# An attention kernel in which VectorE, not GpSimd, adds the norm's bias to the normalised rows

## What is computed

```python
def _layernorm(x, axis=-1, eps=1e-05):
    m = jnp.mean(x, axis=axis, keepdims=True)
    v = jnp.var(x, axis=axis, keepdims=True)
    return (x - m) / jnp.sqrt(v + eps)
...
    # _L0_attn_ref, on the normalised x
    tok = x.reshape(B, H * W // C, C)
...
    att = jnp.concatenate([x1, x2], axis=-1) @ proj_w + proj_b
    mu = att.mean(-1, keepdims=True)
    var = ((att - mu) ** 2).mean(-1, keepdims=True)
    normed = (att - mu) * lax.rsqrt(var + EPS) * ln_w + ln_b
    tok = tok + normed
    return jnp.transpose(tok, (0, 2, 1)).reshape(B, H, W)
...
    x = x + _layernorm(_L0_attn_ref(_layernorm(x, axis=-1), ...), axis=-1)
    x = x + _layernorm(_L0_ffn_ref(_layernorm(x, axis=-1), ...), axis=-1)
```

## Time and profile before

| | us |
|---|---|
| median of three executions | 1118.66 |
| lowest and highest | 1116.5, 1118.77 |
| the profiled execution | 1114.17 |
| its span | 1112.0 |
| TensorE (PE) busy | 932.1 |
| VectorE (DVE) busy | 890.0 |
| GpSimd (POOL) busy | 697.9 |
| ScalarE (ACT) busy | 603.9 |

### The profile page before, as it was taken

One profiled execution on the slowest core, in us unless ns is written; L12 is line 12 of the kernel. 1 busy time (PEld: TensorE's weight loads), 2 busy tenths in 40 slices (PEclk: granted clock), 3 DMA queues, 4 the chain that ended last, 5 costly groups with the idle time before them and its releaser, 6 DMA issues.

```text
span 1112.0 us, 13901 instructions
## 1 busy us (share of the span) xinstructions
PE 932.1 (84%) x4423; PEld 511.2 (46%) x4423; DVE 890.0 (80%) x1135; ACT 603.9 (54%) x907; POOL 697.9 (63%) x497
## 2 busy tenths in 40 slices
PE   5633538999889988999899988999899979889995
PEld 4432424555445544554445545454455543434442
DVE  4999997899798988899789988899889989642213
ACT  2546646655385646756475747655565635523422
POOL 2556555777479755876578756976487757632422
PEclk9856869999899999999999999999999999999997
DMA  6000310004002300023002400122002300230101
GB/s 163 22 17 3 97 37 16 16 23 115 1 1 76 95 20 0 22 73 94 0 0 75 113 0 0 48 81 59 1 1 76 77 0 1 76 76 1 38 1 38
DMA packets 78441, 45.93 MB, mean 41 GB/s; under 512 B 39616, under 2 KB 72384, under 8 KB 78400
## 3 DMA queue, kind: packets, MB, share of 16 engines
q1 hardware_dynamic: 73536, 45.10, 14.4%
q10 hardware_dynamic: 4864, 0.32, 0.3%
HBM read 28.63 MB, written 16.78 MB: 41 GB/s over the span
## 4 chain that ended last, share of the span: by engine, by line
PE 26%; DVE 26%; issue 17%; POOL 16%; ACT 13%; POOLq 0%; DVEq 0%; ACTq 0%
DVE prod L1088 10%; PE ps_gate L632 8%; PE ps_up L632 5%; PE ps_acc L656 4%; POOL sum L929 4%; PE ps_w L597 3%; POOL flo L982 3%; POOL xl L900 2%; DVE probs L1097 2%; ACT xb L736 2%; POOL o L977 2%; DVE attn L1097 2%; DVE xlo L1214 1%; POOL frs L885 1%; DVE fuse L1221 1%
## 5 line engine op out<-in xcount | busy, mean ns | idle before, releaser
L1088 DVE TENSOR_TENSOR prod<-ps_x,qkvl 128x2048 f32<-128x2048 f32 x128 | 290.5, 2282 | 8.2 <-ACT ps_x L761 7.7
L632 PE MATMUL ps_gate<-xhi,wg 128*128 128x512 f16 x512 | 198.7, 388 | 21.4 <-DVE xlo L1214 12.0
L982 POOL TENSOR_TENSOR flo<-fuse,fhi 128x512 f16<-128x512 f32 x128 | 148.9, 1166 | 92.4 <-ACT fhi L829 92.2
L632 PE MATMUL ps_up<-xhi,wu 128*128 128x512 f16 x512 | 196.3, 383 | 8.7 <-DVE fuse L1221 8.7
L632 PE MATMUL ps_gate<-xlo,wg 128*128 128x512 f16 x512 | 198.9, 388 | 0.0
L920 POOL TENSOR_TENSOR sum<-prod 128x1024 f32<-128x1024 f32 x64 | 150.7, 2361 | 75.6 <-DVE prod L1088 54.7
L632 PE MATMUL ps_up<-xlo,wu 128*128 128x512 f16 x512 | 195.7, 382 | 0.0
L929 POOL TENSOR_TENSOR sum<-prod 128x1024 f32<-128x1024 f32 x64 | 151.3, 2369 | 67.3 <-DVE prod L1088 66.2
L823 ACT ACTIVATE gact<-ps_gate,sgate 128x512 f32<-128x512 f32 x128 | 87.5, 684 | 157.3 <-PE ps_gate L632 156.9
L1221 DVE SCALAR_TENSOR_TENSOR fuse<-ps_up,sup,gact 128x512 f32<-128x512 f32 x128 | 95.4, 746 | 95.1 <-PE ps_up L632 78.8
L597 PE MATMUL ps_w<-wqkvl,xt 128*128 128x256 f32 x448 | 123.6, 401 | 24.2 <-ACT xt L743 16.5
(11 more groups left out here) (168 smaller groups left out, 1451.5 us busy)
## 6 DMA issues: line engine op xcount, KB each, us to landing
xb<-in_L_attn_x SPq DMA_DIRECT2D x64, 128.0 KB, 2.7
xr<-in_L_attn_x SPq DMA_DIRECT2D x16, 512.0 KB
attn_rows<-ratt SPq DMA_DIRECT2D x16, 512.0 KB, 3.7
o<-attn_rows SPq DMA_DIRECT2D x32, 256.0 KB, 4.2
out_x<-o SPq DMA_DIRECT2D x14, 512.0 KB
x<-in_L_ffn_w_gate SPq DMA_DIRECT2D x1, 1024.0 KB, 5.5
xr<-in_L_ffn_w_up SPq DMA_DIRECT2D x1, 1024.0 KB, 8.3
out_x<-o SPq DMA_DIRECT2D x4, 256.0 KB
```

Source lines behind the costliest of these rows:

```text
L632: mm = nc.tensor.matmul(ps[:], w[:, k, :], xs[:, k, :], start=(k == 0 and part == 0), stop=(k == KB - 1 and part == 1))
L982: nc.gpsimd.tensor_tensor(flo[:, m % SPLITS, :], fuse[:, m % 2, :], fhi[:, m % SPLITS, :], ALU.subtract).then_inc(flo_done, 1)
L1088: nc.vector.tensor_tensor(prod[:, half].rearrange("p (s j k) -> p s j k", j=WIN, k=WIN), left[:, :, None, :].broadcast_to([P, 4 * WIN, WIN ...
```

## The change

The function token_bias moves from GpSimd's block to VectorE's, with the same waits and the same semaphore at its end. Its place in the list of steps stays. VectorE comes to it where its own order has it, 16 times in all.

```diff
@@ in @block.gpsimd @@
-            def token_bias(at, bank):
-                t, g = at
-                pool.wait_ge(xn_done, WIN * t + WIN)
-                if isinstance(t, int) and at == (0, 1):
-                    pool.wait_ge(xn1_done, WIN)
-                need(pool, ratt_done, 4 * t + 2 * g - 2)
-                nc.gpsimd.tensor_tensor(xl[:, g].rearrange("p h (c t) -> p h c t", c=C),
-                                        xb[:, g, 0:WIN, :].rearrange("p h (c t) -> p h c t", c=C),
-                                        lnb[:, None, :, None].broadcast_to([P, WIN, C, WIN]),
-                                        ALU.add).then_inc(xl_done, 4)
...
-            walk(pool, {"ln1_fin": ln1_fin, "token_bias": token_bias_first, "qk": qk, "pv": pv, "attn_out": attn_add,
+            walk(pool, {"ln1_fin": ln1_fin, "qk": qk, "pv": pv, "attn_out": attn_add,
...
@@ in @block.vector @@
+            def token_bias(at, bank):
+                t, g = at
+                dve.wait_ge(xn_done, WIN * t + WIN)
+                if isinstance(t, int) and at == (0, 1):
+                    dve.wait_ge(xn1_done, WIN)
+                need(dve, ratt_done, 4 * t + 2 * g - 2)
+                nc.vector.tensor_tensor(xl[:, g].rearrange("p h (c t) -> p h c t", c=C),
+                                        xb[:, g, 0:WIN, :].rearrange("p h (c t) -> p h c t", c=C),
+                                        lnb[:, None, :, None].broadcast_to([P, WIN, C, WIN]),
+                                        ALU.add).then_inc(xl_done, 4)
+
+            def token_bias_first(at, bank):
+                if isinstance(at[0], int) and at == (0, 0):
+                    dve.wait_ge(s_const2, 16 * LATER)
+                token_bias(at, bank)
```

More of the change, by code:

```diff
@@ L1017, in _ @@
                                         pattern=[[-2, P // 2], [0, 2]], channel_multiplier=1).then_inc(setup_pool, 1)
[L1019 to L1022, removed]
             def cent_out_first(at, bank):
@@ L1345, in _ @@
                        "finish": finish, "blocks": blocks, "scale_sums": scale_sums, "scale_pow2": scale_pow2,
-                       "scales": scales, "finish_last": finish_last, "finish_add_last": finish_add_last})
+                       "scales": scales, "finish_last": finish_last, "finish_add_last": finish_add_last,
+                       "token_bias": token_bias_first})
 _INS = ["L0_attn_x", "L0_attn_qkv_w", "L0_attn_conv_w0", "L0_attn_conv_b0", "L0_attn_conv_w1", "L0_attn_conv_b1",
```

## The result

| | before | after |
|---|---|---|
| median, us | 1118.72 (4 runs) | 1155.03 (4 runs) |
| lowest and highest | 1116.5, 1118.89 | 1152.66, 1156.04 |
| the profiled execution | 1114.17 | 1152.66 |
| its span | 1112.0 | 1150.9 |

A forecast was written before the change was run, and what follows sets the result against it. No engine is full; three engines handing work on in fixed orders set the 123.0 us pass. Start 6.7 plus six passes' halves 28.0 gave +34.7 us on 1118.66, so 1153.4 us; range 1131 to 1161.

The forecast's parts named there:

- The likeliest case: The forecast of 1153.4 us, with additions held by GpSimd's sums on the shared port; chance 0.68.
- GpSimd has the port first at the second half: GpSimd's sum starts before VectorE's second-half addition and holds it; with the subtraction held too, +3.64 us in each of six passes.
- The rival with VectorE first: VectorE gets the port first at the second half: +0.3 us per pass instead of +3.64, total 1133.4 us; chance 0.15.
- Held for whole instructions: VectorE operations with two SBUF inputs and GpSimd operations wait for each other's whole instruction; some 0.13 us of start-up overlaps.
- The rival without holding: The moved addition is not held, only as long as it is: sum 18.4 us, total 1137 us; chance 0.09.
- The second effect: At the second half, GpSimd's next sum starts right at the product's end and holds the softmax subtraction to 629.85.
- First half: First-half addition in six loop passes: held by GpSimd's sum, then holding flo, which holds the subtraction; +1.03 us each.
- The start: The four additions of the first two tiles, once each: 2.9 + 1.2 + 1.8 + 0.8 = 6.7 us.
- The fourth addition: Last of the first two tiles' additions, partly in 0.23 us of idle time before xlo at 161.64; +0.8 us.
- TensorE's slow stretches: Gate matmuls slowed by TensorE's clock behind a pause: one more per pass adds 7.8 us, giving the upper end, 1161.
- the first four lines of the table: Forecast: first two additions 4.1, third and fourth 1.8 + 0.8, first halves 6.2, second halves 21.8 us.
- the stretches between: Time between a second half and the next first half, where the change has no instruction; forecast 0.

The follow-up runs named there:

- sum_yields: The changed kernel, but in tiles 2 to 7 GpSimd's first pv sum also waits until VectorE's second-half addition is done; 1134.31 us, ratio 1.0167.
- psum_input: The changed kernel, but the twelve additions of tiles 2 to 7 read ps_x in PSUM instead of the bias in SBUF; 1139.26 us, ratio 1.0217.
- first_only: Against the kernel before, only the six first-half additions of tiles 2 to 7 move to VectorE; 1124.07 us, ratio 1.0088.
- moved_gpsimd: The kernel before, all additions on GpSimd, the first-half one of tiles 2 to 7 moved behind norm1_add; 1117.97 us, ratio 1.0021.
- delay_2: The kernel before, with eight of tile 1's statistics repeated on VectorE, 64 us from the start; 1118.63 us, ratio 1.0020.

## Why the prediction was right, and where it was off

The forecast of 1153.4 us lies 1.6 below the measured median, and its ratio (34.7 of 1118.66, 3.1%) lies inside the measured interval. The likeliest case was the one that came, and its mechanism is the one that the traces show.

- **GpSimd has the port first at the second half.** Right, and this decided most: 21.6 us measured, 21.8 forecast. The rows of before showed a start 0.09 us ahead for the sum; it was 0.19 in the trace after, since VectorE began 0.14 us behind ratt's end and not 0.04. The rival with VectorE first (+0.3 per pass) is what sum_yields made of it: 0.42 to 0.66.
- **Held for whole instructions.** Right: 1.82 and 3.27 us for the additions (forecast 1.7 to 1.8 and 3.3 to 3.4), 2.35 for the subtraction behind the second (2.4). The rival without holding falls with psum_input.
- **The second effect,** the next sum in front of the subtraction, was right: it is the 1.5 to 1.6 us that psum_input keeps at each second half.
- **First half.** 0.97 to 0.99 for 1.03 in five passes, but 0.18 in the first, in first_only too; why the first is smaller is not shown. The working gives 577.54 - 576.53 = 1.01, and the sum took 1.03. The term was 1.1 us too large in sum. That GpSimd's saved time buys nothing was right (idle 2.83, forecast 2.9; moved_gpsimd).
- **The start.** The eight rows start 4.59 us later (forecast 4.5) and TensorE's first products 3.11 (2.9). What was too small is the step behind these: I let all behind them follow as they stood. The first three groups of four products took 2.08, 1.91 and 1.89 us and the fourth 1.04, where before they took 2.07, 1.79 and then already 1.03. VectorE's first product is 4.01 late, and the first ssum 5.15, for 4.1 forecast. The fourth addition gave 0.35 for 0.8.
- **TensorE's slow stretches.** This is the term that was off most. I booked them as the upper end only ("one more such slow stretch per pass would add 1.3 x 6 = 7.8 us if nothing covered it") and not in the sum. In the profiled execution they came in three passes with 1.4 to 1.7 us each and in one with 0.7, together 5.6 with the two small steps. As a bound the term was of the right size; as a value, zero was wrong there. The six passes held fourteen low stretches instead of six, and the four that fell shortly ahead of a pass's first ssum cost time. Why there are more is open: a later start and the longer waits within a pass both remain possible. By the medians less is left for them. The 36.3 us less the first four lines of the table (34.0) leave 2.3.
- **Busy times.** "GpSimd's busy time down by 38 us" was wrong: 25.0. The same sentence says that held time counts as busy, but counts it for VectorE alone; GpSimd's flo is held as well, 12.0 us in all, and my own working had flo end 1 us later at each first half.
- **Why it comes out so near all the same.** In the profiled executions the difference is 38.5 against 34.7. By the medians it is 36.3, since the profiled execution of before (1114.17) is faster than all four of its timed ones. A part of the agreement is therefore luck of about 2 us. In the table, too, the misses partly cancel: the first halves came 1.1 below their term and the stretches between 5.6 above.

## What to carry to other kernels

Before an operation with two inputs in SBUF goes to VectorE, look in both timelines at what GpSimd runs at each of its places: the price here was not its length but who started first there, and which instruction with the same need stood behind it. The place in the list was worth over half of the cost of this change (21.4 of 36.3 us), so try the neighbouring places, or a wait that settles who goes first, before giving up the move or keeping it. And an engine's share of the chain of waits is a gain only if the engine, rid of the work, does not simply wait longer for the same thing: here GpSimd waited 2.83 us in place of 0.45.

## What the runs showed of the hardware that was not expected

- Both sides are held, and the holding passes to and fro: in one first half the sum held the addition (0.6 us), the addition flo (1.0), and flo the subtraction (0.25). The profile books all of it as busy time of the one that stands.
- An added wait can make a kernel faster: sum_yields differs from the change in one wait of GpSimd, and its ratio is 1.0167 instead of 1.0326.
- TensorE's granted clock falls to its lower level (0.50 to 0.51) for short stretches within a steady loop, and where they fall in a pass depends on more than the instructions of that pass: in delay_2 the same 547 matmuls took 112.17 us and the pass 123.0, or 113.76 and 124.8. Parts of a change measured one by one therefore did not add up (4.5% against 3.3%), while their steps did.
- At the start TensorE's products ran at half pace until 25.8 us before and until 30.7 after. The view of after puts a granted clock of 1.00 beside this stretch, but that is no measurement: the trace's records of the clock begin only at 25.7 us before and at 30.7 after, with the higher level, just where the pace doubles. So the lower level held them by all appearance, and no record shows it. Of after, the stretch at half pace by busy time:

```profile
25.40:30.60 5.20, 5.20 (x13) 4.18 (x13) 1.11 (x6) 1.19 (x2) 0.00 (x0) 1.00 0.00 0
```

Thirteen matmuls fill 5.20 us there, 0.40 each; in the loop four like them take 1.03 to 1.13 at the higher level and 2.08 at the lower (713.51 above), started 0.22 apart at the higher.
